# Decoder layer on one core: the running decay products of a half formed in one block, its z and o rows scaled by one instruction each

## The chip, the cores and the metric

The kernel runs on 1 core of one Trainium2 chip. The metric is the time of one execution on the device, in microseconds. The time before is the median of 3 runs, 2566.19 us, with 2550.21 as the lowest and 2579.52 as the highest.

## The reference, cut to what matters

The reference is one decoder layer on 16 sequences of 128 tokens and width 256: a gated linear attention with a recurrent state, a long convolution against a context, and a mixture of 64 experts, each followed by a layer norm. The change lies in the recurrence of the first part. For each sequence, head (16) and step it is this, with a state `St` of 128 x 128:

```
def step(St, inp):
    kt, qt, vt, at, bt = inp
    Sk = jnp.einsum('bhij,bhj->bhi', St, kt)
    err = Sk - vt
    Sn = at[..., None] * St - (bt[..., None] * err)[..., None] * kt[:, :, None, :]
    ot = jnp.einsum('bhij,bhj->bhi', Sn, qt)
    return (Sn, ot)
```

`at` is a decay of its own for every row i of the state and every step, from a sigmoid.

## The kernel before, in words

The kernel works in stages, one after the other: `projections`, `recurrence` (lines 439 to 1078), the output of the attention, the long convolution, the experts. Only `recurrence` is touched.

**Tiling.** The 256 pairs of sequence and head are split in GR = 2 groups of 128, which lie in the 128 partitions. The 128 steps are cut in NCHUNK = 8 chunks of C = 16 steps. One chunk of one group is a *leaf*: 16 leaves, numbered at = c * 2 + g, run one after the other, and the two groups alternate. A leaf has two halves of HALF = 8 steps. The state is never formed. What is kept is a row per past step (`u`, 128 columns) with the decays since. Products of two steps' k and q vectors come ready from `projections` (`gram`, in tile `gd`).

**Tiles.** `zo[g]` has two planes of 16 rows by 128 columns: plane 0 is z, what older steps give to S k, plane 1 is o, what they give to the output. `dec[half]` has the decays of a half. `pp` has their running products, row k being dec[0] * ... * dec[k]. `ws` and `w[g]` have the new rows of steps 0 to k with their decays up to k.

**VectorE (DVE) per leaf** (lines 610 to 747). Step k of a half (`step`, from line 647) multiplies row k of z by pp[k-1], in half 0 forms pp[k], then decays all k old rows at once (line 666, called w(k) in the prediction), adds k of them to z with a gram factor each (lines 668 to 680), and makes the new row (lines 682 to 684, called u(k)). After steps 3 and 7 of half 0 four rows of o are multiplied by four rows of pp (line 699). Behind half 0 stands the middle (lines 702 to 727): z and o rows of half 1 by pp[7], products of dec[1], scaling of the history that lies on the chip (line 718), then the addition of ps_x to z (line 725). In half 1 the products are there before step 0. Every DVE operation counts `step_done` up, and a later one that reads its result waits for the count (`after`). Ahead of line 666 DVE also waits for `pair_mm` (line 663), PE's count of products taken, since the old rows in `ws` are written over.

**From half 0 to half 1** (the near exchange). After step 7 DVE counts `half_done` (line 697). POOL then sends the 8 new rows by 8 DMAs (`send_rows`, line 768). PE multiplies them (`near_product`), ACT copies, PE turns the result into ps_x (`near_turn`), and DVE adds it at line 725.

**PE and ACT.** ACT builds diagonal matrices of gram factors (line 996), four to a buffer, and PE uses them to sum the output rows (`own_rows`, line 949), k + 1 products for row k, in order, after DVE has made that row. After each four rows PE adds the scaled o rows (line 953), waiting for `scaled_at`. Between the rows of half 0 PE also does the *history units* of the leaf before (`history`, line 908): 16 units of 8 products, 13 of them spread over half 0 by `UNITS_AFTER = (0, 0, 1, 2, 2, 2, 3, 3)`. Their operands (`turned`, `gcol`) are loaded by SP into four buffers. A load waits until the unit four before it is done (`mm_done`), and the newest rows are there only after DVE has ended the leaf (`leaf_done`) and POOL has stored them (`store_u`, line 795). Their sums come back from DRAM as z and o of the group's next leaf (`load_sums`, line 788). Leaves 0 and 15 have no history units.

Of the kernel before, what the change touches and what calls it, by code (L numbers as in the profile page):

```python
# [25 lines left out]
P = 128  # L26
B, T, D = 16, 128, 256
H, DH = 16, 128
# [410 lines left out]
def recurrence(nc, late, last_out, xT, wgT, woT, a_dram, bv_dram, gram_dram, beta_dram, hist_dram, sums_dram, o_dram):  # L439
# [8 lines left out]
    HALF = C // 2  # L448
# [14 lines left out]
    CHAINS = 4  # L463
    CONSTS = 5
    BLANK_O = CONSTS + 1
# [3 lines left out]
    with ExitStack() as ctx:  # L469
        m = Pool(nc, ctx)  # L470
        hist = [m.sb("p2_hist0", [P, OLD, DH])[:], late[:].rearrange("p (r i) -> p r i", i=DH)]
        zo = [m.sb(f"p2_zo{g}", [P, 2, C, DH]) for g in range(GR)]
        dec = [m.sb(f"p2_dec{half}", [P, HALF, DH]) for half in range(2)]
# [4 lines left out]
        pp = m.sb("p2_pp", [P, HALF, DH])  # L478
# [49 lines left out]

        def step_ops(half, k):

            return (1 + k if k else 0) + (1 if k >= CHAINS else 0) + (1 if half == 0 else 0) + (1 if k else 0) + 1

        def scale_ops(half, k):

            return 0 if k % 4 != 3 else 1 if half == 0 else 3 if k == 3 else 0

        MIDDLE = 2 + 1 + HALF + 1 + 2
        HALF_STEPS = [sum(step_ops(half, k) + scale_ops(half, k) for k in range(HALF)) for half in range(2)]
        STEPS = sum(HALF_STEPS) + MIDDLE + 1

        def rows_at(at, s):

            half, k = divmod(s, HALF)
            before = (HALF_STEPS[0] + MIDDLE) * half + sum(step_ops(half, x) + scale_ops(half, x) for x in range(k))
            return at * STEPS + before + step_ops(half, k)

        def scaled_at(at, bank):

            half, k = bank // 2, 3 if bank > 1 else bank * 4 + 3
            return rows_at(at, half * HALF + k) + scale_ops(half, k)  # L550

        def pairs_at(at, s):

# [53 lines left out]
        def _(dve):  # L607
            nc.vector.memset(zo[0][:, 0], 0.0).then_inc(zo_zero, 1)

            def leaf(c, g):  # L610
# [4 lines left out]
                def done(ins):  # L615
                    count[0] += 1
                    ins.then_inc(step_done, 1)
                    return count[0]

                def after(n):  # L620
                    if n:
                        dve.wait_ge(step_done, base + n)

                def mul(out, in0, in1):
                    return done(nc.vector.tensor_tensor(out=out, in0=in0, in1=in1, op=ALU.mult))  # L625
# [18 lines left out]
                if c:  # L644
                    dve.wait_ge(zo_in[g], c * (2 * DMA))

                def step(half, k, p_at, w_at, u_at):

                    s = half * HALF + k
                    z = zo[g][:, 0, s, :]  # L650
                    new = state(g, s)
                    z_at = 0
                    if k:
                        old, side = state(g, s - 1), zo[g][:, 0, s - 1, :]
                        after(p_at)
                        z_at = mul(z, z, pp[:, k - 1, :])
                    if half == 0:
                        if k == 0:
                            p_at = done(nc.vector.tensor_copy(pp[:, 0, :], dec[0][:, 0, :]))
                        else:  # L660
                            p_at = mul(pp[:, k, :], pp[:, k - 1, :], dec[0][:, k, :])
                    if k < HALF - 1 and (at + half or k >= STATE_BEHIND[k]):
                        dve.wait_ge(pair_mm, state_free(at, s))
                    if k:
# [18 lines left out]
                        out=new[:, k, :], in0=z, scalar=beta[g][:, s:s + 1], in1=w[g][:, 1 + s, :],  # L683
                        op0=ALU.mult, op1=ALU.subtract, reverse1=True))
                    assert base + u_at == rows_at(at, s), (u_at, rows_at(at, s) - base)
                    return p_at, w_at, u_at

                p_at = w_at = u_at = o_at = 0
                for k in range(HALF):
                    p_at, w_at, u_at = step(0, k, p_at, w_at, u_at)  # L690
                    if k % 4 == 3:
                        after(p_at)
                        if at == 0:
                            dve.wait_ge(cleared, BLANK_O)
                        if k == HALF - 1:
                            after(u_at)
                            dve.sem_inc(half_done, 1)  # L697
                        rows = slice(k - 3, k + 1)
                        o_at = mul(zo[g][:, 1, rows, :], zo[g][:, 1, rows, :], pp[:, rows, :])
                        assert base + o_at == scaled_at(at, k // 4)  # L700

                after(o_at)
                for f in range(2):
                    h_at = mul(zo[g][:, f, HALF:, :], zo[g][:, f, HALF:, :], pp[:, HALF - 1:HALF, :].broadcast_to([P, HALF, DH]))
                w_at = done(nc.vector.tensor_copy(w[g][:, 0, :], pp[:, HALF - 1, :]))
                dve.wait_ge(hi_in, c * (GR * DMA) + (g + 1) * DMA)
                after(w_at)
# [17 lines left out]
                    z_at = add(zo[g][:, 0, rows, :], zo[g][:, 0, rows, :], ps_x[:, q])  # L725
                after(z_at)
                dve.sem_inc(x_read, 1)
                w_at = u_at = 0
                p_at = z_at
                for k in range(HALF):  # L730
                    p_at, w_at, u_at = step(1, k, p_at, w_at, u_at)
                    if k == 3:
                        dve.wait_ge(x_done, at * BANKS + BANKS)
                        for q in range(2):
                            rows = slice(HALF + q * 4, HALF + q * 4 + 4)
                            o_at = add(zo[g][:, 1, rows, :], zo[g][:, 1, rows, :], ps_x[:, q])
                        after(o_at)
                        dve.sem_inc(x_read, 1)
                        o_at = mul(zo[g][:, 1, HALF:, :], zo[g][:, 1, HALF:, :], pp[:])
                        assert base + o_at == scaled_at(at, 2)  # L740
# [1606 lines left out]
```

## Time and profile before

| | |
|---|---|
| median of 3 runs | 2566.19 us |
| lowest, highest | 2550.21, 2579.52 us |
| the profiled execution | 2562.71 us |
| its span, first to last instruction | 2561.1 us |
| mean granted TensorE clock | 0.871 |
| DVE busy | 1776.5 us (69%), 4427 instructions |
| PE busy | 2007.7 us (78%), 12402 matrix products |
| ACT busy | 1174.8 us (46%) |
| recurrence | from 662 to 1778 us of the span |

Busy time is the sum of the time in which an engine worked on an instruction. An engine can be busy and yet not set the end. So for a change in one stage the waits in that stage say more: which engine stood still, for how long, and what ended it. DMA share is the mean busy share of the 16 DMA engines.

### The profile page before, as it was taken

The numbers are of one execution on the slowest core, as the hardware profiler recorded it, in microseconds if no ns is written. First come the engines' busy times: TensorE is split into PE (matmuls) and PEld (weight loads), VectorE is DVE, ScalarE is ACT, GpSimd is POOL, SyncE is SP. The second block draws the span as 40 slices with busy tenths as digits, with TensorE's granted clock in tenths as the row PEclk, the third lists the DMA queues.
The fourth block names the chain that finished last, engine by engine and source line by source line (L and its number), as shares of the span: only waits on it lengthen the run. The fifth ranks groups of instructions, "written<-read, shape, count | busy, mean of one in ns | idle before, by whom it ended". The sixth has DMA issues, their size and how long they took to land. (4 is left out here: it accounts for less than half of the span.)

```text
span 2561.1 us, 40464 instructions
## 1 busy us (share of the span) xinstructions
PE 2007.7 (78%) x12402; PEld 1368.8 (53%) x12402; DVE 1776.5 (69%) x4427; ACT 1174.8 (46%) x2737; POOL 944.5 (37%) x969
## 2 busy tenths in 40 slices
PE   7999999999477777666665654476999948899994
PEld 4444444444355555554544543354788833566763
DVE  4888888887678778777876866666656517774444
ACT  2655666565356656555554533453333210323442
POOL 1444444444433223322222212211444436345774
PEclk8999999999688887877777776787999979899996
DMA  2666666666457889999999998974322251107985
GB/s 85 129 122 128 127 123 123 127 128 120 104 135 197 212 219 244 240 233 259 287 284 278 298 268 250 288 205 156 99 66 74 87 204 33 57 26 234 315 216 147
DMA packets 641632, 443.55 MB, mean 173 GB/s; under 512 B 294997, under 2 KB 594981, under 8 KB 636197
## 3 DMA queue, kind: packets, MB, share of 16 engines
q1 hardware_dynamic: 526536, 271.03, 41.1%
q0 software_dynamic: 40672, 128.75, 19.2%
q10 hardware_dynamic: 74240, 41.58, 5.7%
q8 instruction: 83, 1.36, 0.2%
q14 instruction: 101, 0.83, 0.1%
HBM read 238.76 MB, written 194.04 MB: 169 GB/s over the span
## 5 line engine op out<-in xcount | busy, mean ns | idle before, releaser
L996 ACT ACTIVATE p_diag_o<-p_ident,p_gd 128x128 f32<-128x128 f32 x1152 | 360.9, 389 | 328.4 <-PE p_ps_o L949 309.0
L398 DVE SCALAR_TENSOR_TENSOR p_y<-p_ps_proj,p_w,p_y 128x508 f32<-128x508 f32 (+2 forms) x576 | 416.1, 741 | 113.9 <-ACT p_y L310 100.4
L949 PE MATMUL p_ps_o<-p_ws,p_diag_o 128*128 128x128 f32 x1792 | 326.5, 345 | 143.7 <-ACT p_diag_o L996 68.0
L949 PEld LDWEIGHTS p_ps_o<-p_ws,p_diag_o 128*128 128x128 f32 x1792 | 291.0, 247 | 202.1 <-ACT p_diag_o L996 75.2
L243 PE MATMUL p_ps_proj<-p_x,p_w 128*128 128x512 f32 x768 | 342.9, 596 | 2.7 <-ACT p_beta_t L301 2.7
L908 PE MATMUL p_ps_z<-p_turned,p_gcol 112*32 112x128 f32 x3584 | 148.8, 307 | 226.8 <-DMA p_turned<-history 226.8
L206 POOL TENSOR_TENSOR p_kq<-p_y,p_sig 128x512 f32<-128x512 f32 x128 | 162.2, 1270 | 357.3 <-ACT p_sig L321 356.4
L908 PEld LDWEIGHTS p_ps_z<-p_turned,p_gcol 112*32 112x32 f32 x3584 | 101.0, 121 | 285.3 <-DMA p_turned<-history 244.6
L631 DVE SCALAR_TENSOR_TENSOR p_zo<-p_ws,p_gd,p_zo 128x128 f32<-128x128 f32 x768 | 240.0, 347 | 3.5
L243 PEld LDWEIGHTS p_ps_proj<-p_x,p_w 128*128 128x128 f32 x768 | 142.1, 192 | 158.0 <-issue 155.0
L775 POOL DMA_DIRECT2D p_near_t<-gram x128 | 67.0, 548 | 317.1 <-PE p_ps_x L933 314.3
L310 ACT ACTIVATE p_y<-p_ps_proj,p_w 128x512 f32<-128x512 f32 x192 | 149.2, 777 | 62.9 <-PE p_ps_proj L243 58.0
L625 DVE TENSOR_TENSOR p_ws<-p_ws,p_dec 128x128 f32<-128x128 f32 (+2 forms) x192 | 118.8, 619 | 79.8 <-PE p_ps_o L949 79.8
L625 DVE TENSOR_TENSOR p_zo<-p_zo,p_pp 128x128 f32<-128x128 f32 (+2 forms) x304 | 140.6, 475 | 5.2 <-DVE p_w L682 0.2
L628 DVE TENSOR_TENSOR p_zo<-p_zo,p_ps_x 128x512 f32<-128x512 f32 x64 | 41.0, 682 | 133.0 <-PE p_ps_x L933 133.0
L1234 PE MATMUL p_ps_g<-p_late 128*128 (+1 forms) x512 | 115.9, 386 | 11.6 <-POOL p_ident L1193 9.6
L768 POOL DMA_DIRECT2D p_near_w<-p_w x128 | 67.1, 545 | 150.7 <-DVEq L697 150.1
L321 ACT ACTIVATE p_sig<-p_y 128x512 f32<-128x512 f32 x192 | 119.4, 623 | 4.4 <-issue 3.4
L253 PE MATMUL p_ps_a<-p_wa,p_x 128*128 (+1 forms) x256 | 120.3, 592 | 0.0
L1487 PE MATMUL p_ps_y<-p_prod,p_toep 128*128 128x512 f32 x192 | 89.5, 617 | 35.4 <-DMA p_toep<-filters 25.6
L333 ACT ACTIVATE p_gram<-p_ps_gram 128x512 f32<-128x512 f32 x128 | 69.5, 595 | 99.9 <-PE p_ps_v L271 99.9
L1254 PE MATMUL p_ps_o<-p_late,p_y 128*128 128x256 f32 x512 | 113.6, 383 | 2.0 <-POOL p_y L1204 2.0
(263 smaller groups left out, 3837.2 us busy)
## 6 DMA issues: line engine op xcount, KB each, us to landing
p_w<-in_wguT SPq DMA_DIRECT2D x64, 480.0 KB
history_sums<-p_sums ACTq DMA_DIRECT2D x112, 256.0 KB, 6.2
p_zo<-history_sums POOLq DMA_DIRECT2D x28, 1024.0 KB, 11.4
history<-p_hist SPq DMA_DIRECT2D x9, 2048.0 KB, 12.5
history<-p_late SPq DMA_DIRECT2D x9, 2048.0 KB, 13.5
decays<-p_dec SPq DMA_DIRECT2D x64, 256.0 KB, 2.3
beta_v<-p_bv SPq DMA_DIRECT2D x64, 256.0 KB, 2.5
gram<-p_gram SPq DMA_DIRECT2D x64, 256.0 KB, 3.7
```

The lines of the kernel that those rows point to most:

```text
L206: nc.gpsimd.tensor_tensor(out=dst, in0=y[u % 4][:].rearrange("p (b t) -> p b t", b=QB), in1=sig[u % 2][:].rearrange("p (b t) -> p b t", b=QB),
L243: last = nc.tensor.matmul(ps_proj[u % 4][:], w_sb[j % 2][:, k, kind, :], x_sb[:, k, n * 512:(n + 1) * 512], start=(k == 0), stop=(k == KT ...
L253: nc.tensor.matmul(ps_a[:].rearrange("p h i -> p (h i)"), x_sb[:, k, t0:t0 + T], wa_sb[:, k, heads], start=(k == 0), stop=False)
L310: nc.scalar.activation(y[u % 4][:], ps_proj[u % 4][:], ACT.Identity, bias=par[j % 2][:, kind, TAPS:TAPS + 1], scale=par[j % 2][:, kind, TA ...
L321: nc.scalar.activation(sig[u % 2][:], y[u % 4][:], ACT.Sigmoid).then_inc(sig_done, 1)
L398: nc.vector.scalar_tensor_tensor(out=yv[:, :, s:], in0=pv[:, :, 0:T - s], scalar=par[j % 2][:, kind, TAPS - 1 - s:TAPS - s], in1=yv[:, :, ...
L625: return done(nc.vector.tensor_tensor(out=out, in0=in0, in1=in1, op=ALU.mult))
L631: return done(nc.vector.scalar_tensor_tensor(out=acc, in0=row, scalar=scalar, in1=acc, op0=ALU.mult, op1=ALU.add))
L908: last = nc.tensor.matmul(ps_z[k % NZ][h * 2 * C:(h + 1) * 2 * C, u % UB * QUADS + q, :], gcol[n % NTURN][:, q * 4 + h, :], turned[n % NTU ...
L949: nc.tensor.matmul(ps_o[s // 4 % 2][:, s % 4, :], diag_o[p // DO % NDO][:, p % DO, :], rows[:, r, :], start=(s % 4 == 0 and r == 0), stop= ...
L996: last = nc.scalar.activation(diag_o[n % NDO][:, p % DO, :], ident[:], ACT.Copy, scale=gd[g][:, r, s:s + 1])
L1234: last = nc.tensor.matmul(ps_g[g % 2][:, e, :], wg[:, k, (2 * g + e) * DH:(2 * g + e + 1) * DH], xT_sb[:, k, bass.ds(p * (PB * T), PB * T) ...
```

## The change

The running products of half 0 are all formed right behind the first new row, in a chain of one copy and seven multiplies. Rows 1 to 7 of z are then scaled by one multiply, and all 8 rows of o by another, ahead of step 1. `step` no longer scales z nor forms products. In the middle, z and o rows of half 1 are multiplied by pp[7] in one instruction instead of two. In half 1 rows 1 to 7 of z are scaled by one multiply behind the first new row. The counts that PE waits for (`rows_at`, `scaled_at`) follow the new order. Instructions per leaf: 7 z multiplies become 1 in each half, 2 o multiplies become 1, 2 multiplies of the middle become 1.

```
--- before.py
+++ after.py
@@ -528,13 +528,13 @@
 
         def step_ops(half, k):
 
-            return (1 + k if k else 0) + (1 if k >= CHAINS else 0) + (1 if half == 0 else 0) + (1 if k else 0) + 1
+            return (1 + k if k else 0) + (1 if k >= CHAINS else 0) + 1 + (0 if k else 1 if half else HALF + 2)
 
         def scale_ops(half, k):
 
-            return 0 if k % 4 != 3 else 1 if half == 0 else 3 if k == 3 else 0
-
-        MIDDLE = 2 + 1 + HALF + 1 + 2
+            return 3 if half and k == 3 else 0
+
+        MIDDLE = 1 + 1 + HALF + 1 + 2
         HALF_STEPS = [sum(step_ops(half, k) + scale_ops(half, k) for k in range(HALF)) for half in range(2)]
         STEPS = sum(HALF_STEPS) + MIDDLE + 1
 
@@ -542,12 +542,13 @@
 
             half, k = divmod(s, HALF)
             before = (HALF_STEPS[0] + MIDDLE) * half + sum(step_ops(half, x) + scale_ops(half, x) for x in range(k))
-            return at * STEPS + before + step_ops(half, k)
+            return at * STEPS + before + (step_ops(half, k) if k else 1)
 
         def scaled_at(at, bank):
 
-            half, k = bank // 2, 3 if bank > 1 else bank * 4 + 3
-            return rows_at(at, half * HALF + k) + scale_ops(half, k)
+            if bank < 2:
+                return at * STEPS + step_ops(0, 0)
+            return rows_at(at, HALF + 3) + scale_ops(1, 3)
 
         def pairs_at(at, s):
 
@@ -644,21 +645,13 @@
                 if c:
                     dve.wait_ge(zo_in[g], c * (2 * DMA))
 
-                def step(half, k, p_at, w_at, u_at):
+                def step(half, k, z_at, w_at, u_at):
 
                     s = half * HALF + k
                     z = zo[g][:, 0, s, :]
                     new = state(g, s)
-                    z_at = 0
                     if k:
                         old, side = state(g, s - 1), zo[g][:, 0, s - 1, :]
-                        after(p_at)
-                        z_at = mul(z, z, pp[:, k - 1, :])
-                    if half == 0:
-                        if k == 0:
-                            p_at = done(nc.vector.tensor_copy(pp[:, 0, :], dec[0][:, 0, :]))
-                        else:
-                            p_at = mul(pp[:, k, :], pp[:, k - 1, :], dec[0][:, k, :])
                     if k < HALF - 1 and (at + half or k >= STATE_BEHIND[k]):
                         dve.wait_ge(pair_mm, state_free(at, s))
                     if k:
@@ -683,25 +676,26 @@
                         out=new[:, k, :], in0=z, scalar=beta[g][:, s:s + 1], in1=w[g][:, 1 + s, :],
                         op0=ALU.mult, op1=ALU.subtract, reverse1=True))
                     assert base + u_at == rows_at(at, s), (u_at, rows_at(at, s) - base)
-                    return p_at, w_at, u_at
-
-                p_at = w_at = u_at = o_at = 0
-                for k in range(HALF):
-                    p_at, w_at, u_at = step(0, k, p_at, w_at, u_at)
-                    if k % 4 == 3:
-                        after(p_at)
-                        if at == 0:
-                            dve.wait_ge(cleared, BLANK_O)
-                        if k == HALF - 1:
-                            after(u_at)
-                            dve.sem_inc(half_done, 1)
-                        rows = slice(k - 3, k + 1)
-                        o_at = mul(zo[g][:, 1, rows, :], zo[g][:, 1, rows, :], pp[:, rows, :])
-                        assert base + o_at == scaled_at(at, k // 4)
-
-                after(o_at)
-                for f in range(2):
-                    h_at = mul(zo[g][:, f, HALF:, :], zo[g][:, f, HALF:, :], pp[:, HALF - 1:HALF, :].broadcast_to([P, HALF, DH]))
+                    return w_at, u_at
+
+                w_at, u_at = step(0, 0, 0, 0, 0)
+                p_at = done(nc.vector.tensor_copy(pp[:, 0, :], dec[0][:, 0, :]))
+                for k in range(1, HALF):
+                    after(p_at)
+                    p_at = mul(pp[:, k, :], pp[:, k - 1, :], dec[0][:, k, :])
+                after(p_at)
+                z_at = mul(zo[g][:, 0, 1:HALF, :], zo[g][:, 0, 1:HALF, :], pp[:, 0:HALF - 1, :])
+                if at == 0:
+                    dve.wait_ge(cleared, BLANK_O)
+                o_at = mul(zo[g][:, 1, 0:HALF, :], zo[g][:, 1, 0:HALF, :], pp[:])
+                assert base + o_at == scaled_at(at, 0)
+                for k in range(1, HALF):
+                    w_at, u_at = step(0, k, z_at, w_at, u_at)
+                after(u_at)
+                dve.sem_inc(half_done, 1)
+
+                h_at = mul(zo[g][:, :, HALF:, :], zo[g][:, :, HALF:, :],
+                           pp[:, HALF - 1:HALF, :].unsqueeze(1).broadcast_to([P, 2, HALF, DH]))
                 w_at = done(nc.vector.tensor_copy(w[g][:, 0, :], pp[:, HALF - 1, :]))
                 dve.wait_ge(hi_in, c * (GR * DMA) + (g + 1) * DMA)
                 after(w_at)
@@ -725,10 +719,10 @@
                     z_at = add(zo[g][:, 0, rows, :], zo[g][:, 0, rows, :], ps_x[:, q])
                 after(z_at)
                 dve.sem_inc(x_read, 1)
-                w_at = u_at = 0
-                p_at = z_at
-                for k in range(HALF):
-                    p_at, w_at, u_at = step(1, k, p_at, w_at, u_at)
+                w_at, u_at = step(1, 0, 0, 0, 0)
+                z_at = mul(zo[g][:, 0, HALF + 1:, :], zo[g][:, 0, HALF + 1:, :], pp[:, 0:HALF - 1, :])
+                for k in range(1, HALF):
+                    w_at, u_at = step(1, k, z_at, w_at, u_at)
                     if k == 3:
                         dve.wait_ge(x_done, at * BANKS + BANKS)
                         for q in range(2):
```

## Rows read from the trace of the kernel before

**Rows 1.** Busy time by stretch, leaves 0, 1, 13: length; PE, PEld, DVE, ACT, POOL; clock; DMA share; GB/s

```profile
662.41:719.22 56.81, 36.62 (x183) 30.14 (x183) 51.41 (x136) 34.44 (x108) 19.38 (x32) 0.69 0.19 46
719.22:781.15 61.93, 45.96 (x464) 37.39 (x464) 46.77 (x136) 38.59 (x110) 19.14 (x33) 0.83 0.67 173
...
1546.97:1635.92 88.95, 47.55 (x453) 38.26 (x453) 60.42 (x140) 35.44 (x102) 19.07 (x34) 0.69 0.94 264
```

**Rows 2.** Waits, 660 to 1790: who waited for what; us in total, times, longest

```profile
PE p_ps_z L908 <- DMA p_turned<-history: 226.8, 65, 26.0
...
DVE p_zo L628 <- PE p_ps_x L933: 133.0, 16, 17.0
...
DVE p_ws L625 <- PE p_ps_o L949: 79.8, 7, 22.5
```

**Rows 3.** Timeline of leaf 1, PE, then DVE: start, us, operation, count, [idle before]

```profile
727.52 0.65 PE L908 MATMUL p_ps_z<-p_turned,p_gcol 112*32 112x128 f32 x16 [3.79 <-DMA p_turned<-history]
728.10 1.79 PE L949 MATMUL p_ps_o<-p_ws,p_diag_o 128*128 128x128 f32 x8
...
738.20 0.67 PE L908 MATMUL p_ps_z<-p_turned,p_gcol 112*32 112x128 f32 x16 [3.98 <-DMA p_turned<-history]
...
750.26 0.94 PE L949 MATMUL p_ps_o<-p_w,p_diag_o 128*128 128x128 f32 x6
...
738.48 0.35 DVE L682 SCALAR_TENSOR_TENSOR p_w<-p_zo,p_beta,p_w 128x128 f32<-128x128 f32 x1
```

**Rows 4.** Timeline at the end of half 0: leaf 0 on DVE, leaf 15 on PE

```profile
686.30 0.35 DVE L682 SCALAR_TENSOR_TENSOR p_w<-p_zo,p_beta,p_w 128x128 f32<-128x128 f32 x1
...
696.17 1.29 DVE L628 TENSOR_TENSOR p_zo<-p_zo,p_ps_x 128x512 f32<-128x512 f32 x2 [3.07 <-PE p_ps_x L933]
...
1750.68 1.16 PE L922 MATMUL p_ps_n<-p_near_g,p_near_w 128*128 128x128 f32 x8 [0.31 <-DMA p_near_w<-p_w]
```

**Rows 5.** Timeline of DVE: start of half 1 of leaf 0, start of leaf 1

```profile
697.61 0.35 DVE L682 SCALAR_TENSOR_TENSOR p_ws<-p_zo,p_beta,p_w 128x128 f32<-128x128 f32 x1
697.88 0.29 DVE L625 TENSOR_TENSOR p_zo<-p_zo,p_pp 128x128 f32<-128x128 f32 x1
698.08 0.28 DVE L625 TENSOR_TENSOR p_ws<-p_ws,p_dec 128x128 f32<-128x128 f32 x1
...
719.22 0.23 DVE L659 COPY p_pp<-p_dec 128x128 f32<-128x128 f32 x1 [0.34 <-DVE p_zo L625]
719.36 0.35 DVE L682 SCALAR_TENSOR_TENSOR p_ws<-p_zo,p_beta,p_w 128x128 f32<-128x128 f32 x1
...
720.03 0.29 DVE L625 TENSOR_TENSOR p_ws<-p_ws,p_dec 128x128 f32<-128x128 f32 x1
...
722.39 0.35 DVE L682 SCALAR_TENSOR_TENSOR p_ws<-p_zo,p_beta,p_w 128x128 f32<-128x128 f32 x1
```

**Rows 6.** Timeline of DVE: multiplies of other sizes, dependent ones, leaves 0 to 2

```profile
686.90 3.09 DVE L625 TENSOR_TENSOR p_zo<-p_zo,p_pp 128x512 f32<-128x512 f32 x3 [0.24 <-DVE p_w L682]
...
704.02 1.43 DVE L625 TENSOR_TENSOR p_zo<-p_zo,p_pp 128x1024 f32<-128x1024 f32 x2
...
714.05 1.08 DVE L625 TENSOR_TENSOR p_w<-p_ws,p_dec 128x896 f32<-128x896 f32 x1
...
717.27 0.35 DVE L682 SCALAR_TENSOR_TENSOR p_w<-p_zo,p_beta,p_w 128x128 f32<-128x128 f32 x1
717.66 1.22 DVE L625 TENSOR_TENSOR p_zo<-p_w,p_pp 128x1024 f32<-128x1024 f32 x1
...
724.96 0.89 DVE L625 TENSOR_TENSOR p_zo<-p_zo,p_pp 128x512 f32<-128x512 f32 x2
...
742.55 2.25 DVE L625 TENSOR_TENSOR p_pp<-p_pp,p_dec 128x128 f32<-128x128 f32 x7
...
807.08 2.29 DVE L718 TENSOR_TENSOR p_hist<-p_hist,p_zo 128x2048 f32<-128x2048 f32 x1
```

**Rows 7.** Timeline of DVE, leaf 8, step 6 of half 0

```profile
1187.57 0.96 DVE L625 TENSOR_TENSOR p_ws<-p_ws,p_dec 128x768 f32<-128x768 f32 x1 [2.95 <-PE p_ps_o L949]
```

## The prediction

> **What bounds the kernel now.** I read the stretches by leaf first. The recurrence runs from 662 to 1778 us of the span in 16 leaves, one stretch each, of which three are shown [rows 1]. Leaf 0 takes 57 us at a DMA share of 0.19, leaf 1 takes 62 us at 0.67, leaf 13 takes 89 us at 0.94. DVE is busy for 51, 47 and 60 us of these, so what grows in the later leaves is not DVE's work.
>
> The view of waits says what each engine stood still for [rows 2]. DVE waited for ps_x (L628, the step from half 0 to half 1) once a leaf, 133.0 us together. In 7 leaves it waited at k = 6 of half 0 until PE had read old state rows, 79.8 us. PE itself waited 226.8 us for history rows to land.
>
> One leaf, in order of time, shows how these hang together [rows 3]. Leaf 1 starts at 719.22. DVE starts u(7), the last row of half 0, at 738.48. PE is behind it: its first history unit waits for DMA until 727.52, a later one until 738.20, and row 7 is reached only at 750.26. The near products and ps_x come behind that. Leaf 0 has no history units, and there ps_x follows u(7) in 9.9 us (686.30 to 696.17). Leaf 15 has none either: PE's last wait ahead of ps_x is for near_w, which POOL sends as soon as half 0 ends [rows 4].
>
> So the path through leaves 1 to 14 is: end of the leaf on DVE, store of its new rows, history loads, PE's units, near products, ps_x, half 1 on DVE. Half 0 on DVE lies beside it. In leaves 0 and 15 both halves are on the path.
>
> **The change part by part.** What counts on DVE is the distance from start to start, since neighbours overlap. A 128-column multiply lasts 0.29 us, but an independent one behind it starts after 0.20, which is 0.08 before its end (697.88 to 698.08). I use 0.08 for the long ones too. An independent instruction behind a row result starts 0.27 after it (697.61 to 697.88) [rows 5].
>
> *Half 0, up to w(1), the decay of the state in step 1.* Now the copy is at 719.22, u(0) at 719.36 and w(1) at 720.03, 0.81 us from the leaf's start [rows 5]. After the change u(0) is first, the copy 0.27 later, the first product 0.27 behind the copy (its 0.23 and 0.04 for the wait), and the seven dependent products take 2.25 with 0.04 for the wait behind them, 2.29. The z multiply of 896 columns takes 1.08 - 0.08 = 1.00, as the one at 714.05. The o multiply of 1024 columns takes 1.15: the two at 704.02, of 128 and 1024 columns, take 1.43, less 0.20 and 0.08 [rows 6]. The sum is 0.27 + 0.27 + 2.29 + 1.00 + 1.15 = 4.98, so w(1) is 4.17 later.
>
> *Half 0, steps 2 to 7.* Each loses a z multiply and a product between u(k-1) and w(k). They did not cost their 0.40: w(k) reads what u(k-1) wrote, and they covered that wait. Now u to w is 0.67 (719.36 to 720.03) [rows 5]. A direct dependence of this kind is the row result at 717.27 that the multiply at 717.66 reads: 0.39 [rows 6]. So a step gets 0.28 back, six of them 1.68. The o multiply behind step 3 goes too. It and a z multiply take 0.89 (724.96), less 0.08 and 0.20: 0.61 [rows 6]. u(7), and with it the signal to POOL, comes 4.17 - 1.68 - 0.61 = 1.88 us later.
>
> *Middle.* Three multiplies, 3.09 us at 686.90, (one of 512 and two of 1024 columns) become one of 2048, for which the history multiply of 2048 columns stands with 2.29 [rows 6]. That is 0.80 back, so the middle ends 1.08 later than now. It lies under the wait for ps_x, which is 3.07 us in leaf 0 and longer in most. I count nothing. If that cover were gone it would cost 1.08.
>
> *Half 1.* Now u(0) to w(1) is 0.47 [rows 5]. After the change it is 0.27 + 1.00 = 1.27, 0.80 more. Steps 2, 3, 5, 6 and 7 go from 0.47 to 0.39, which gives 0.40 back. Step 4 stands behind the o multiply and not behind u, and gets 0.20 back. Half 1 is 0.20 us longer.
>
> So there are 14 instructions fewer a leaf, and DVE's chain still gets longer. The products and z multiplies stood where something had to be waited for anyway, and now they stand in a block by themselves.
>
> The Trainium skill, Vector Engine (DVE) Microarchitecture Reference, section 5.2 on measured stream behaviour, gives a fixed cost of about 75 ns per instruction beside 1.04 ns a column. By that alone 14 fewer would save 1.05 us a leaf, 17 us in all and a time of 2546 (an estimate from that page). The trace agrees with the size for independent neighbours, 0.20 us for 128 columns, and shows nothing saved where the next one reads the result.
>
> *Who waits for what is late.* In leaf 1 PE takes row 2 before unit 0. u(2) starts 3.17 us after the leaf now (722.39) and would start at 3.17 + 4.17 - 0.28 = 7.06. With 0.4 for its result and 0.7 for PE's six records of it that is 8.2, against 8.30 when unit 0 came (727.52): hidden, with nothing to spare. u(3) starts at 5.47 now (0.27 ahead of 724.96) and would at 9.08. PE's row 3 goes from 8.88 (728.10) to 9.5, 0.6 late [rows 3, 5, 6]. The row itself is covered by PE's next DMA wait, 3.98 us. But behind it stand units 1 and 2, whose end lets SP issue the loads of units 5 and 6. I take half of the 0.6, in the six leaves where unit 0 comes this early: 1.8 us, with bounds 0 and 3.6. u(7) has 11.8 us of room (738.48 against 750.26) and uses 1.9. In leaves 8 to 14 the lateness at k = 6 is 4.17 - 5 x 0.28 - 0.61 = 2.16, less than the smallest wait there, 2.95 [rows 7]. No DMA is moved past a queue. POOL's near_w sends stand behind the signal of half 0 and start 1.88 later. What is queued behind them, the next decays and near loads, isn't needed before the next leaf.
>
> *Sum.* Leaves 0 and 15: 2 x (1.88 + 0.20) = 4.2. Leaves 1 to 14: 14 x 0.20 = 2.8. Loads: 1.8. Together 8.8 us on the profiled execution's 2562.7, which gives 2571.5, +0.35%. That execution lies 3.5 us under the median of the runs (2566.2, from 2550.2 to 2579.5). About 1% is what a measurement of this kernel tells from no change.
>
> **The bounds of the one price that matters**, u to w. Below: 0.27, the distance of two independent instructions. Above: 0.60, as from 686.30 to 686.90, where the signal to POOL stands between row and multiply [rows 4, 6]. I take 0.39, the case with nothing between. The wait for PE's count that stands ahead of w(k) can be met while u runs.
>
> **The rivals.**
>
> *All freed slots come back* (u to w at 0.27). Half 1 becomes 6 x 0.20 - 0.80 = 0.40 shorter, and half 0 late by 4.17 - 6 x 0.40 - 0.61 = 1.16. The sum is 2 x 0.76 - 14 x 0.40 = -4.1: 2559 us. For it speaks the shorter queue. Against it: w(k) reads u(k-1)'s row and waits for its semaphore. Chance 0.14, within 1%.
>
> *Half 0 is exposed in every leaf.* If PE came to wait for DVE's rows rather than for history loads, it would be 16 x 2.08 = 33 us: 2596, +1.3%. It decides from the point where u(3) or u(7) reaches PE later than the DMA wait behind it ends. For it: rows 2 and 3 are at PE within 0.1 and 0.6 us of that. Against it: 3.98 us of DMA wait behind them, and 11.8 us at row 7. Chance 0.09.
>
> *u to w costs 0.60.* Half 1 becomes 0.80 + 5 x 0.13 - 0.20 = 1.25 longer, half 0 4.17 - 6 x 0.07 - 0.61 = 3.14. The sum is 14 x 1.25 + 2 x 4.39 = 26.3, with the loads 2591, +1.1%. For it: no row shows the wait for PE's count uncovered, right behind u. Against it: a wait that is met costs nothing beside a running instruction. Chance 0.07.
>
> *Faster by over 1%* takes 1.6 us off every leaf. Half 1, the one part of DVE on the path of 14 leaves, gives 0.4 at best. What is left is a shift of history loads against other transfers in the leaves with DMA near 1, which I can't work out. Chance 0.10.
>
> **How the numbers follow.** The forecast has 0.60, at 2572 us. Within 1% are the forecast and the first rival, 0.74. Slower by over 1% has 0.16, faster 0.10. The range goes down to 2550, which is the first rival less the 9 us by which single runs scatter here, and up to 2596, the exposed case.
>
> **What would show it.** In the changed profile: leaf start to u(7) in leaf 1 at 21.1 us instead of 19.26, w(1) 5.0 behind the start, u to w 0.39. DVE's busy time down by 2.1 us a leaf (1.08 for seven of 0.29, twice, and two large ones merged), while from ps_x to the leaf's end it takes 0.2 more. PE in half 0 still waiting for history, not for state rows. The prediction is wrong if leaves 1 to 7 grow by 2 us each, or if half 1 gets shorter.

## The result and the profile after

| | before | after |
|---|---|---|
| median of 20 runs each | 2563.61 us | 2572.23 us |
| lowest, highest | 2538.35, 2588.42 | 2559.01, 2583.28 |
| ratio to before, 95% interval | | 1.0043 [1.0025, 1.0061] |
| the profiled execution | 2562.71 us | 2582.22 us |

The change costs 0.43%, 11 us of 2563.61 (6 to 16 by the interval). The ratio leaves out three slow runs of the kernel before, more than 1.5% above its fastest; over all 20 runs of each the medians are 8.6 us apart and the means 10.0. That is less than the 1% that one set of runs tells from no change, and it is seen only because there are 20 runs of each.

The two profiled executions are 19.5 us apart, more than the medians. In them leaf 15 ends 30.9 us later (1776.06 and 1806.98), and the stages behind it, whose code is the same, take 11.4 us less (785.0 and 773.6; all the profiles of this document have 771 to 785 there). So lengths within the recurrence are compared, not the spans, and no single profile prices the change.

First DVE, leaf 0's half 1 and leaf 1's start in the changed kernel, the places of [rows 5, 6]. Columns: start, us, operation, count, what ended the idle time before.

```profile
702.12 0.35 DVE L675 SCALAR_TENSOR_TENSOR p_ws<-p_zo,p_beta,p_w 128x128 f32<-128x128 f32 x1
702.39 1.08 DVE L626 TENSOR_TENSOR p_zo<-p_zo,p_pp 128x896 f32<-128x896 f32 x1
703.39 0.28 DVE L626 TENSOR_TENSOR p_ws<-p_ws,p_dec 128x128 f32<-128x128 f32 x1
...
718.66 0.35 DVE L675 SCALAR_TENSOR_TENSOR p_ws<-p_zo,p_beta,p_w 128x128 f32<-128x128 f32 x1
719.04 1.09 DVE L626 TENSOR_TENSOR p_w<-p_ws,p_dec 128x896 f32<-128x896 f32 x1
...
722.65 1.22 DVE L626 TENSOR_TENSOR p_zo<-p_w,p_pp 128x1024 f32<-128x1024 f32 x1
724.29 0.35 DVE L675 SCALAR_TENSOR_TENSOR p_ws<-p_zo,p_beta,p_w 128x128 f32<-128x128 f32 x1 [0.41 <-PE p_ps_o L943]
724.56 0.62 DVE L682 COPY p_pp<-p_dec 128x128 f32<-128x128 f32 x1
...
727.49 2.23 DVE L626 TENSOR_TENSOR p_zo<-p_zo,p_pp 128x896 f32<-128x896 f32 x2
729.63 0.28 DVE L626 TENSOR_TENSOR p_ws<-p_ws,p_dec 128x128 f32<-128x128 f32 x1
...
730.22 0.35 DVE L675 SCALAR_TENSOR_TENSOR p_ws<-p_zo,p_beta,p_w 128x128 f32<-128x128 f32 x1
730.67 0.42 DVE L626 TENSOR_TENSOR p_ws<-p_ws,p_dec 128x256 f32<-128x256 f32 x1
...
746.15 0.35 DVE L675 SCALAR_TENSOR_TENSOR p_w<-p_zo,p_beta,p_w 128x128 f32<-128x128 f32 x1
746.64 2.29 DVE L626 TENSOR_TENSOR p_zo<-p_zo,p_pp 128x2048 f32<-128x2048 f32 x1
```

The block is there: 702.39 is the z multiply of 896 columns in half 1, and w(1) follows 1.00 later. From the end of leaf 0's work (722.65 + 1.22 = 723.87) to u(7) of leaf 1 it takes 22.28 us. Before it was 717.66 + 1.22 = 718.88 to 738.48 [rows 3, 6], 19.60. So half 0 is 2.68 longer, not 1.88. Two things were mis-sized. u to w is 0.45 where the wait for PE's count stands between (730.22 to 730.67) and 0.38 where it does not (718.66 to 719.04, k = 7). And the copy lasted 0.62 instead of 0.23. Five steps of 0.06 or 0.07, 0.39 for the copy and 0.08 at the start make the 0.80.

That is the price in leaves 1 to 7, where the copy lasted 0.62 or 0.65. Leaves 0 and 15, the two in which the prediction has half 0 on the path, pay less. In leaf 0 u(0) to u(7) takes 25.38 us instead of 23.75, 1.63 more, because DVE stands still behind POOL at its start in both kernels (last section). In leaf 15 the end of leaf 14 to u(7) takes 21.92 instead of 19.59, 2.33 more.

DVE's busy time in leaf 1 did not fall by the forecast 2.1 us. From leaf end to leaf end, before and then after (columns as in [rows 1]):

```profile
718.88:780.81 61.93, 45.69 (x462) 37.11 (x462) 46.77 (x137) 38.59 (x109) 19.14 (x33) 0.83 0.67 173
```

```profile
723.87:786.70 62.83, 46.05 (x463) 37.41 (x462) 47.95 (x123) 38.93 (x110) 19.18 (x33) 0.84 0.68 171
```

There are 14 instructions fewer and 1.18 us more. This view counts the time of overlapping neighbours once. Added up one by one the durations fell, from 54.4 to 52.7 us, but those taken out had lain partly under their neighbours.

Then PE in leaf 1 of the changed kernel, which answers to [rows 3].

```profile
727.52 0.38 PE L943 MATMUL p_ps_o<-p_ws,p_diag_o 128*128 128x128 f32 x2
730.62 1.23 PE L943 MATMUL p_ps_o<-p_ws,p_diag_o 128*128 128x128 f32 x4 [2.72 <-DVE p_ws L675]
732.19 1.65 PE L943 MATMUL p_ps_o<-p_ws,p_diag_o 128*128 128x128 f32 x6 [0.34 <-DVE p_ws L675]
733.77 1.08 PE L902 MATMUL p_ps_z<-p_turned,p_gcol 112*32 112x128 f32 x16
...
744.42 2.28 PE L902 MATMUL p_ps_z<-p_turned,p_gcol 112*32 112x128 f32 x32 [4.16 <-DMA p_turned<-history]
...
755.66 2.05 PE L943 MATMUL p_ps_o<-p_w,p_diag_o 128*128 128x128 f32 x16
```

PE now waits for DVE at row 1 (2.72 us), and unit 0 starts without a wait for its data. A long wait for history still follows (4.16 us, until 744.42), and row 7 comes at 755.66, 9.5 us after DVE has started it. Counted from the end of the leaf before, unit 0 comes at 9.90 us instead of 8.64, the end of that later wait at 20.55 instead of 19.32, row 7 at 31.79 instead of 31.38, and ps_x at 39.63 instead of 39.23. So a third of the 1.26 us by which unit 0 is late is left at ps_x.

The waits of the recurrence in the changed kernel answer to [rows 2]. The window is 660 to 1800, in which the kernel before has the same 226.8 and 133.0. Columns: who waited for what, us in total, times, longest.

```profile
PE p_ps_z L902 <- DMA p_turned<-history: 184.6, 55, 22.9
...
DVE p_zo L629 <- PE p_ps_x L927: 141.6, 16, 17.8
...
PE p_ps_o L943 <- DVE p_ws L675: 88.8, 71, 7.7
```

The last of these in the kernel before:

```profile
PE p_ps_o L949 <- DVE p_ws L682: 55.7, 46, 24.2
```

PE's wait for history fell by 42.2, from 226.8 to 184.6, and its wait for DVE's rows rose by 33.1, from 55.7 to 88.8. One wait took the place of part of the other.

Worked out of the two timelines by leaf, in us. The end of a leaf is the end of its multiply of 1024 columns from w, and ps_x is the start of DVE's first addition of it.

```
leaf                          1     2     3     7     12    15
before: end to ps_x         39.2  39.1  39.3  48.3  63.2  29.0
after:  end to ps_x         39.6  41.3  41.8  45.1  63.6  34.0
before: ps_x to end         22.7  22.7  22.7  22.7  22.7  22.7
after:  ps_x to end         23.2  23.2  23.2  23.2  23.2  23.4
```

Half 1 is 0.49 longer in nearly every leaf (22.70 to 23.20), against 0.20 forecast. From end to ps_x single leaves scatter from run to run in every kernel: leaf 12, 63.2 here, took 50.6 in the run `p_half1` below.

Leaves 1 to 7 together took 450.4 us before, 451.0 and 451.9 in `p_half1` and `p_middle`, which leave half 0 as it was. With the block of half 0 they took 461.6 in the changed kernel, 464.2 in `copy_first`, 452.4 in `wait_ahead` and 452.2 in `p_half0`. In the first three, half 1 has 3.5 of that. So what half 0 costs there goes from nothing to some 10 us, 1.5 us a leaf, from one profiled execution to the next, and why it differs is not known.

### The profile page after: what moved, and what is told of

Read it like the earlier page. It is cut to its first block and busy times, and to the rows that moved or that the text cites. A ratio compares the mean times of both kernels' runs of the same rounds, so it can differ in the third digit from the quotient of the medians.

```text
span 2580.6 us, 40253 instructions
## 1 busy us (share of the span) xinstructions
PE 2023.7 (78%) x12402; PEld 1381.9 (54%) x12402; DVE 1789.8 (69%) x4203; ACT 1176.1 (46%) x2737; POOL 945.9 (37%) x969
## 5 line engine op out<-in xcount | busy, mean ns | idle before, releaser
L943 PE MATMUL p_ps_o<-p_ws,p_diag_o 128*128 128x128 f32 x1792 | 344.5, 354 | 189.1 <-DVE p_ws L675 88.0
L943 PEld LDWEIGHTS p_ps_o<-p_ws,p_diag_o 128*128 128x128 f32 x1792 | 302.1, 253 | 253.6 <-DVE p_ws L675 104.7
L902 PE MATMUL p_ps_z<-p_turned,p_gcol 112*32 112x128 f32 x3584 | 154.5, 315 | 184.9 <-DMA p_turned<-history 184.6
L626 DVE TENSOR_TENSOR p_zo<-p_zo,p_pp 128x896 f32<-128x896 f32 (+2 forms) x80 | 109.3, 1383 | 5.2
```

The costliest lines, as they stand in the source:

```text
L902: last = nc.tensor.matmul(ps_z[k % NZ][h * 2 * C:(h + 1) * 2 * C, u % UB * QUADS + q, :], gcol[n % NTURN][:, q * 4 + h, :], turned[n % NTU ...
L943: nc.tensor.matmul(ps_o[s // 4 % 2][:, s % 4, :], diag_o[p // DO % NDO][:, p % DO, :], rows[:, r, :], start=(s % 4 == 0 and r == 0), stop= ...
```

## The experiments

All ratios are to the kernel before, run on the same chip, with 95% intervals. The first four (`p_half0`, `p_half1`, `p_middle`, `o_late`) ran on one chip, `d_early`, `d_half1`, `o_move` and `o_late_move` on a second, the others on a third. Ratios of different groups meet only through the kernel before.

**The parts alone.** `p_half0` is the kernel before with the block of half 0 of the diff above, and `z_at` in `step` only for half 1:

```
                    if k:
                        old, side = state(g, s - 1), zo[g][:, 0, s - 1, :]
+                       if half:
                            after(p_at)
                            z_at = mul(z, z, pp[:, k - 1, :])
```

> The kernel before with the half 0 part of the change alone: products in one chain, z and o rows scaled by one multiply each, ahead of step 1. Half 1 and the middle as before. The changed kernel's trace has u(0) to u(7) at 21.9 us instead of 19.1, 2.7 more. Path theory (half 0 lies beside PE's history units in leaves 1 to 14): 2 x 2.7 = 5.4 us for leaves 0 and 15, and up to 1 us a leaf in leaves 1 to 7 where rows 1 to 3 reach PE late: 5 to 12 us, ratio 1.002 to 1.005. Rival (half 0 exposed everywhere): 16 x 2.7 = 43 us, ratio 1.017.

Measured: 1.0068 [1.0038, 1.0098], 17 us (10 to 25). u(0) to u(7) is 21.9 us as expected, half 1 stays at 22.70. The upper case of 43 us is out. The cost is above the 5 to 12 us expected, with an interval that reaches into it.

`p_half1` has the other block:

```
+               _, w_at, u_at = step(1, 0, 0, 0, 0)
+               z1_at = mul(zo[g][:, 0, HALF + 1:, :], zo[g][:, 0, HALF + 1:, :], pp[:, 0:HALF - 1, :])
+               for k in range(1, HALF):
+                   _, w_at, u_at = step(1, k, z1_at, w_at, u_at)
```

> The kernel before with the half 1 part alone: rows 1 to 7 of z scaled by one multiply behind the first new row. The changed kernel's trace has ps_x to the leaf's end at 23.20 us instead of 22.70. Path theory (half 1 is on the path of every leaf): 16 x 0.49 = 8 us, ratio 1.003. Rival (DMA sets leaves 5 to 14, their half 1 is covered): 6 x 0.49 = 3 us, ratio 1.001. Rival (fewer instructions are what counts): below 1.

Measured: 1.0031 [0.9999, 1.0063]. ps_x to end is 23.19, the 0.49 expected. The interval holds both the 8 and the 3 us. That fewer instructions pay is not borne out.

`p_middle` has the multiply of both planes by `pp[:, HALF - 1:HALF, :].unsqueeze(1).broadcast_to([P, 2, HALF, DH])`.

> The kernel before with the merged multiply of the middle alone (one of 2048 columns for two of 1024). Both theories: 0.1 us a leaf less DVE work under the wait for ps_x, ratio 1.000. DVE's wait for ps_x grows by 0.1 a leaf.

Measured: 1.0025 [0.9998, 1.0051]. This holds 1.000 and says no more. The three parts add up to 1.24% with an uncertainty of about 0.5, the whole change has 0.43. By the medians of all runs it is 0.53, 0.15 and 0.33, together 1.01%. The three share one set of runs of the kernel before, so an error in that set counts three times. The parts don't add up well, and why stays open.

**Where time counts.** Ten useless dependent multiplies, 4.6 us, were put in at three places in turn:

```
+                   if k == 0:          # d_early; 5 in d_late, and in half 1 (with dec[1]) for d_half1
+                       for _ in range(EXTRA):
+                           after(mul(waste[:], dec[0][:, 0:2, :], dec[0][:, 2:4, :]))
```

> The kernel before with ten useless dependent multiplies of 256 columns (4.6 us) ahead of w(1) in half 0 of each leaf, the place where the change put its block. Path theory: leaves 0 and 15 pay 4.6 each, leaves 1 to 14 pay what rows 2 and 3 are late at PE beyond the next DMA wait, 0 to 2 us: 9 to 37 us, ratio 1.004 to 1.014. Rival (half 0 exposed everywhere): 16 x 4.6 = 74 us, ratio 1.029. Rival (half 0 free but for leaves 0 and 15): 9 us.

Measured: 1.0046 [1.0019, 1.0073], 12 us (5 to 19) of the 74 put in. Half 0 exposed everywhere, 74 us, is out.

> The kernel before with the ten useless multiplies (4.6 us) behind step 5 of half 0 instead of ahead of w(1). Theory (rows 6 and 7 have 10 us of room at PE in leaves 1 to 7, only rows 1 to 3 have none): leaves 0 and 15 pay, 2 x 4.6 = 9 us, ratio 1.0035, and leaves 1 to 7 keep their length. Rival (it is the signal for near_w at the end of half 0 that counts): as d_early, 1.0046 or more.

Measured: 1.0039 [1.0007, 1.0071], 10 us (2 to 18). Early and late cost the same within the intervals, so it is not shown that rows 1 to 3 being late is what leaks. Nor did leaves 1 to 7 keep their length in this trace: together they took 468.1 us against 450.4 (453.2 in `d_early`). The sum is what leaves 0 and 15 pay by themselves, 9 us. Both runs leave room for some more in the other 14 leaves.

> The same ten multiplies (4.6 us) behind step 5 of half 1. Path theory (half 1 on DVE is on the path of every leaf): 16 x 4.6 = 74 us, ratio 1.029. Rival (what loads history late in leaves 1 to 14 hangs on PE's rows and POOL's sends, not on DVE's end; for it speaks that o_late took 2.57 us off half 1 and gained nothing): 15 to 40 us, ratio 1.006 to 1.015.

Measured in 4 runs: 1.0114 [1.0072, 1.0155], 29 us of 74 (18 to 40). The path theory for half 1 falls: 0.4 of what is added shows (0.25 to 0.54). The trace says where the rest goes. In us, from the timelines:

```
leaf                          1     2     11    12    13    14
before:  end to ps_x        39.2  39.1  56.2  63.2  66.4  67.8
d_half1: end to ps_x        40.9  40.4  50.8  49.3  54.0  62.9
before:  whole leaf         61.9  61.8  78.9  85.9  89.1  90.7
d_half1: whole leaf         68.2  67.6  78.1  76.6  81.2  90.2
```

Early leaves pay most of it: leaves 1 to 7 take 477.9 us together instead of 450.4. In leaves 11 to 14 the time from the end to ps_x shrinks by 5 to 14 us, and the leaf gets shorter. Single leaves scatter as much, but leaves 8 to 14 together took 545.3 us against 555.0 before, and 550 to 573 in all other profiles here. These stretches, before and then d_half1, lie mostly in leaf 12 before and in leaves 11 and 12 of d_half1 (columns as in [rows 1]):

```profile
1465.00:1550.00 85.00, 47.66 (x455) 37.99 (x454) 59.65 (x139) 37.37 (x106) 19.27 (x33) 0.72 0.95 270
```

```profile
1465.00:1550.00 85.00, 54.10 (x540) 42.87 (x540) 65.52 (x150) 42.63 (x118) 19.25 (x33) 0.78 1.04 291
```

DMA is busy nearly all the time in both (0.95 and 1.04). I read it so: a longer half 1 is time there in which transfers drain that the next leaf would have waited for. This reading has no run of its own.

**Taking work out of half 1.** `o_late` moves the o rows' additions and multiply behind the end signal, and PE's use of them behind row 15:

```
                 dve.sem_inc(leaf_done, 1)
+                dve.wait_ge(x_done, at * BANKS + BANKS)
+                for q in range(2):
+                    rows = slice(HALF + q * 4, HALF + q * 4 + 4)
+                    o_at = add(zo[g][:, 1, rows, :], zo[g][:, 1, rows, :], ps_x[:, q])
+                after(o_at)
+                dve.sem_inc(x_read, 1)
+                o_at = mul(zo[g][:, 1, HALF:, :], zo[g][:, 1, HALF:, :], pp[:])
...
-                if s % 4 == 3:
+                for s in {3: (3,), 7: (7,), C - 1: (C - 5, C - 1)}.get(s, ()):
                     pe.wait_ge(step_done, scaled_at(at, s // 4))
```

> The kernel before with the o work of half 1 (two additions of ps_x and one multiply of 1024 columns, 2.57 us a leaf) moved from behind step 3 to behind the leaf's end signal, so into half 0 of the next leaf; PE adds the scaled o rows of bank 2 after row 15. Path theory: 2.57 us come off half 1 in leaves 0 to 14 and hide in half 0: 15 x 2.57 = 38 us less, ratio 0.985. Rival (DMA sets leaves 5 to 14): 5 x 2.57 = 13 us less, ratio 0.995. Rival (half 0 exposed everywhere): nothing gained, 1.000.

Measured: 0.9996 [0.9967, 1.0024]. ps_x to end fell from 22.70 to 20.13 as meant, and nothing came of it. My path theory is refuted a second time, from the other side, and the 13 us of the first rival lie outside the interval too. The second rival forecast the 1.000, but its reason, half 0 exposed everywhere, falls with `d_early`. What did not move is POOL's traffic for the leaf after next, here in leaf 2, before and then o_late:

```profile
787.77 1.17 POOL L759 DMA_DIRECT2D heads_out<-p_zo  x1 [4.20 <-issue]
788.93 0.56 POOL L589 DMA_DIRECT2D p_w<-beta_v  x1
789.49 3.37 POOL L593 DMA_DIRECT2D p_gd<-gram  x6
```

```profile
787.81 1.17 POOL L760 DMA_DIRECT2D heads_out<-p_zo  x1 [5.06 <-PE p_ps_o L950]
789.49 0.56 POOL L591 DMA_DIRECT2D p_w<-beta_v  x1 [0.51 <-issue]
790.05 3.38 POOL L595 DMA_DIRECT2D p_gd<-gram  x6
```

These sends wait for PE's last rows and not for DVE's end. They go out just as SP loads the history units (787.29 to 796 before, 786.47 to 796 in o_late). `o_move` puts them behind the near_w sends of the next leaf:

```
                 if at + 1 < LEAVES:
                     load_decays(pool, at + 1, 0, lo_in)
+                if at:
+                    swap(at - 1)       # store_o, load_values, load_grams, load_beta with their waits
+                if at + 1 < LEAVES:
                     load_near(at + 1)
```

> The kernel before with POOL's store of the o rows and its loads of the next values, grams and beta (1 MB each way and 8 gram loads, sent 6 to 16 us into the next leaf) moved behind the near_w sends of the next leaf. Theory: these transfers share the DMA engines with the history loads of units 3 and 4, for which PE waits 4 to 8 us in leaves 1 to 7. Without them the wait shrinks: 2 to 5 us less in each of 6 leaves, 12 to 30 us, ratio 0.988 to 0.995. Rival (the same bytes only collide later, with units 5 to 15 and the history stores): 1.000.

Measured: 0.9947 [0.9925, 0.9970], 14 us less. Leaves 1 and 2 fall from 61.9 and 61.8 us to 54.9 and 56.3. Leaves 1 to 7 together take 422.1 us instead of 450.4, but leaves 8 to 14 take 571.9 instead of 555.0, so part of the rival holds as well: some of the bytes collide later. In leaf 2 the one wait for history ahead of row 7 is that for unit 0:

```profile
785.56 1.08 PE L916 MATMUL p_ps_z<-p_turned,p_gcol 112*32 112x128 f32 x16 [4.51 <-DMA p_turned<-history]
...
789.60 1.08 PE L916 MATMUL p_ps_z<-p_turned,p_gcol 112*32 112x128 f32 x32
...
791.92 1.08 PE L916 MATMUL p_ps_z<-p_turned,p_gcol 112*32 112x128 f32 x32
```

> o_late and o_move together. Theory (in o_late the store of o and the loads behind it stayed at their old time while DVE's end came 2.57 us earlier, and they held the history loads): now the 2.57 us show: 15 x 2.57 = 38 us on top of o_move's gain, ratio 0.975 to 0.98. Rival (half 0 is exposed when it is 2.57 us later against the end signal): the ratio of o_move.

Measured: 0.9915 [0.9886, 0.9943], 22 us less than the kernel before and some 33 less than the changed kernel. It is the fastest here. On top of `o_move` the 2.57 us bring 8 us by the ratios, 5.4 by the medians (2542.31 and 2547.71), and not 38. The two intervals overlap, so this gain is hardly clear of the rival, which had none. Leaves 1 to 7 took 418.2 us (422.1 in `o_move`), leaves 8 to 14 570.3.

> The changed kernel with POOL's sends moved as in o_move (which alone gave 0.9947, leaves 1 to 3 going from 62 to 55 to 59 us, ps_x 12.6 us behind u(7) instead of 19.5). Theory (half 0 of the change is hidden by PE's wait for history units, and with o_move leaves 1 to 4 have only some 2.7 us of it left): the change now costs up to 2.7 us more in 4 leaves beside its 11: ratio to before 1.000 to 1.003. Rival (half 0 stays hidden): 0.9947 + 0.0043 = 0.999.

Measured: 0.9991 [0.9964, 1.0018]. That is the rival's 0.999, and against `o_move` the change costs 0.44% again, with an uncertainty of 0.35 and the two from different chips. The interval also holds most of the theory's 1.000 to 1.003. So it is not shown that half 0 did not become more exposed. The moved sends gain the changed kernel 0.5%, as they gained the kernel before.

**The two sizes.** `copy_first` swaps two lines of the changed kernel:

```
+                p_at = done(nc.vector.tensor_copy(pp[:, 0, :], dec[0][:, 0, :]))
                 w_at, u_at = step(0, 0, 0, 0, 0)
-                p_at = done(nc.vector.tensor_copy(pp[:, 0, :], dec[0][:, 0, :]))
```

> The changed kernel with the copy of the first decay ahead of u(0) again. In the changed kernel's trace this copy, 0.27 behind u(0), lasted 0.62 to 0.65 us in leaves 1 to 7 and ended within 0.04 us of the end of POOL's first send of new rows (724.23 + 0.92 against 724.56 + 0.62). Theory (the copy is held while POOL issues a DMA): ahead of u(0) it starts before POOL's send and lasts 0.23, and u(0) to u(7) falls by 0.27 + 0.4. Rival (the copy is slow right behind a row result): it lasts 0.23 too, but the copies of the middle, which follow no row result, stay at 0.35 where a near_w send runs.

Measured in one execution, the profiled one: u(0) to u(7) is 21.20 instead of 21.89. The copy in leaf 1, and POOL beside it:

```profile
720.22 0.23 DVE L681 COPY p_pp<-p_dec 128x128 f32<-128x128 f32 x1 [0.34 <-DVE p_zo L626]
```

```profile
720.23 0.92 POOL L789 DMA_DIRECT2D history<-p_zo  x1 [14.91 <-DVEq L741]
```

It starts 0.01 ahead of the send and lasts 0.23. The copy of dec[1] in the middle still lasts 0.35 in most leaves, while near_w sends run, though it follows no row result:

```profile
744.59 0.35 DVE L702 COPY p_pp<-p_dec 128x128 f32<-128x128 f32 x1
```

Both speak for the theory.

`wait_ahead` takes the wait for PE's count to the step before:

```
+                    if k + 1 < HALF - 1 and (at + half or k + 1 >= STATE_BEHIND[k + 1]):
+                        dve.wait_ge(pair_mm, state_free(at, s + 1))
                     after(max(z_at, w_at))
                     u_at = done(nc.vector.scalar_tensor_tensor(
```

> The changed kernel with the wait for PE's count moved from between u(k-1) and w(k) to ahead of u(k-1). In the changed kernel's trace u to w is 0.38 where no such wait stands (k = 7, and k = 1 to 3 in the first half of leaf 0) and 0.45 to 0.46 where it does. Theory (a second wait between two dependent instructions costs 0.07): u to w becomes 0.38 in all steps, ps_x to leaf end 23.20 - 0.4 = 22.8, u(0) to u(7) 21.9 - 0.4 = 21.5. Rival (the 0.07 comes from the buffer or the size): stays at 23.2 and 21.9.

Measured in one execution, the profiled one: ps_x to end 23.33 instead of 23.20, u(0) to u(7) 21.84 instead of 21.86. In its trace u to w is 0.38 as expected:

```profile
767.22 0.35 DVE L677 SCALAR_TENSOR_TENSOR p_ws<-p_zo,p_beta,p_w 128x128 f32<-128x128 f32 x1
767.60 0.43 DVE L626 TENSOR_TENSOR p_ws<-p_ws,p_dec 128x256 f32<-128x256 f32 x1
767.95 0.73 DVE L632 SCALAR_TENSOR_TENSOR p_zo<-p_ws,p_gd,p_zo 128x128 f32<-128x128 f32 x2
768.78 0.35 DVE L677 SCALAR_TENSOR_TENSOR p_ws<-p_zo,p_beta,p_w 128x128 f32<-128x128 f32 x1
```

But from the two additions to the next u it is now 0.83 instead of 0.77. The 0.07 moved with the wait and did not go. Half 1 even got 0.13 longer: of its six waits the first and the fourth had stood behind a long multiply and cost nothing there, and now all six stand bare. Half of the theory holds (the second wait is the price), half falls (that it is free elsewhere).

## Why the prediction was right, and where it was not

- **The sign and the time.** 8.8 us more were forecast, 0.35%, and 11 were measured, 0.43% [0.25, 0.61]. The reason given for a longer chain holds as far as the profile shows it: 14 instructions fewer a leaf did not shorten DVE's chain, because those taken out stood in a wait that was there anyway. The way from the chain to the time does not hold, and that the sum came this near is in part luck.
- **Half 0, 1.88 us.** Too small: 2.68. The missing 0.80 is the copy, held 0.39 while POOL issued a send, five steps of u to w at 0.45 instead of 0.39, and 0.08 at the start. In leaves 0 and 15, where the sum used the 1.88, it was 1.63 and 2.33, together 4.0 and by chance close to the 3.8 taken. The forecast has nothing of what evened them out: DVE is held by POOL in leaf 0 in both kernels, and the copy lasts only 0.28 in leaf 15.
- **Half 1, 0.20 us.** Too small: 0.49, by the same u to w. Of the bounds 0.27 and 0.60 the value was nearer to the middle than to the 0.39 taken.
- **Half 0 is covered in leaves 1 to 14.** Right for the most part. Of 74 us put into half 0, 12 and 10 showed, and 9 of these are leaves 0 and 15. The exposed case, 33 us, is out. But "hidden, with nothing to spare" for unit 0 in leaf 1 was off: it comes 1.26 us later, and 0.40 of that reaches ps_x. The sign set for being wrong was 2 us more in each of leaves 1 to 7. They grew by 1.6 us each in the changed kernel's profile, 0.5 of it half 1, and by 0.3 in that of `p_half0`.
- **The loads, 1.8 us.** That term took half of 0.6 us of lateness in six leaves. No run tells it apart. The profiles above allow anything from nothing to 10 us.
- **Half 1 is on the path of leaves 1 to 14, 14 x 0.20.** This step failed. 0.4 of added time shows, and time taken out shows not at all (`o_late`) or to a fifth (8 of 38 us, hardly clear of nothing). In leaves 11 to 14 a DMA share near 1 was in front of me [rows 1], and I counted their half 1 in full all the same. In the early leaves I named the history loads as the path without asking what else was on the DMA engines.
- **The errors offset each other.** The size of half 1 was too small (0.49 for 0.20) and its share too large (0.4 for 1): 16 x 0.49 x 0.4 = 3.1 us, against 16 x 0.20 = 3.2 forecast. That is luck. With 4.0 for half 0 in leaves 0 and 15 this estimate comes to 7 us. It takes the share from 4.6 us added at one place. What is left of the 11, if anything is (the interval begins at 6), would be half 0 in leaves 1 to 14, and that is not shown.
- **All freed slots come back (2559), u to w at 0.60, faster by 1%.** None came. The u to w rival had the right cause in a wait that was no longer covered, at a third of its extra price (0.07 of 0.21).
- The fixed cost per instruction (the Trainium skill, Vector Engine (DVE) Microarchitecture Reference, section 5.2) would have made the changed kernel 17 us faster (an estimate from that page's figure). No run here shows such a gain. A multiply that reads a row result starts 0.38 or more behind it, whatever stands between: 0.38 with nothing, 0.47 with one instruction, 0.67 with two.

## What to carry to other kernels

Before merging small instructions, look at what stands between a result and its reader: an instruction that fills that gap costs little, and taking it out gives back only what is left over. A chain of waits for DMA is not finished at the name of the load that is late: ask what else is sent at that time, and move that first. To learn whether a stretch is on the path, add a known time to it and see what share comes out at the end. And where the DMA share is near 1, as in leaves 8 to 14 here (0.84 to 1.06 before), no change of engine work or of the order of sends visibly paid. They took 555.0 us before, 545.3 with 4.6 us added to half 1, 572.6 with 2.57 taken out of it, 571.9 with the sends moved and 570.3 with both, in profiles that scatter by some 20 us there. Fewer bytes were not tried.

## What the runs showed of the hardware

- A copy of 128 columns on DVE that begins while POOL issues a DMA can be held until that issue ends. In the changed kernel, leaf 1, it is the copy above (724.56 + 0.62 = 725.18) and this send, which ends at 725.15. In leaves 2 to 7 it lasted 0.65 each.

```profile
724.23 0.92 POOL L789 DMA_DIRECT2D history<-p_zo  x1 [14.90 <-DVEq L741]
```

  The multiplies around it were not held. Nor is every copy. In leaf 8 the same copy lasts 0.22 and ends at 1187.94, inside this send, and what tells the two cases apart is open:

```profile
1187.72 0.22 DVE L682 COPY p_pp<-p_dec 128x128 f32<-128x128 f32 x1
...
1187.66 0.57 POOL L587 DMA_DIRECT2D p_dec<-decays  x1
```

  The largest hold is at the start of leaf 0, behind POOL's clearing of tiles. DVE's copy ends 0.08 us after the last of them before (667.42 and 667.34) and 0.09 after it in the changed kernel (669.75 and 669.66):

```profile
662.41 5.01 DVE L659 COPY p_pp<-p_dec 128x128 f32<-128x128 f32 x1 [8.50 <-DMA p_beta<-beta]
...
663.72 3.62 POOL L813 MEMSET p_zo<- 128x4096 f32 x1
```

```profile
665.47 4.28 DVE L682 COPY p_pp<-p_dec 128x128 f32<-128x128 f32 x1
...
666.04 3.62 POOL L807 MEMSET p_zo<- 128x4096 f32 x1
```

  The Trainium skill, SBUF — State Buffer, section "SBUF: two separate sides", describes an exclusive lock on a port pair shared by DVE and GpSimd, which an fp32 copy on DVE takes. The traces agree where a copy is held, from the side on which DVE is the one that waits: 0.39 us of it in leaf 1, some 4 us in leaf 0.
- A second semaphore wait ahead of an instruction that depends on the one before costs 0.06 to 0.07 us (0.45 or 0.46 against 0.38 or 0.39). It is the same in nearly every step and leaf, so it is not PE coming late. It costs the same in front of the neighbouring instruction. With one independent instruction in between it costs nothing: in half 1 of leaf 1 before, row result to multiply is 0.47 at step 7, which has no such wait, and 0.46 or 0.47 at steps 1, 2, 3, 5 and 6, which have it.
